# Mixture-of-experts layer: expert rows scaled by their gates and added by indirect transfers to two DRAM buffers, in place of a gather and combine stage

## The reference, cut to what matters

```python
h = tok(...)                                # (8, 256, 256), a state-space kernel
h = concatenate([h, txt], axis=1)           # (8, 768, 256)
h = h + attn(layernorm(h), Wq, Wk, Wv, Wo)
h = h + ffn(layernorm(h), Wr, br, W1, b1, W2, b2)

def ffn(x, ...):                            # 8 experts, the best 2 per token
    logits = xf @ Wr + br
    topk_w, topk_idx = top_k(logits, 2)
    topk_w = softmax(topk_w)
    gate = sum(one_hot(topk_idx, 8) * topk_w[..., None], axis=1)
    y = relu(xf @ W1[e] + b1[e]) @ W2[e] + b2[e]     # for each expert e
    return einsum('te,eth->th', gate, y)
```

## Time and profile before

| | us |
|---|---|
| median of 3 runs | 2702.7 |
| lowest and highest | 2696.3, 2704.53 |
| profiled execution, its own time | 2709.06 |
| span of that execution, first to last instruction | 2707.3 |

### The profile page before, as it was taken

How to read it: one execution, slowest core, us unless ns; L and a number is a source line. 1 busy time by engine, 2 the same in 40 slices (tenths; PEclk the granted TensorE clock), 3 DMA queues, 4 the chain that set the end, 5 groups by cost and what they waited for, 6 DMA issues and landing times. The chain is left out here.

```text
span 2707.3 us, 59046 instructions
## 1 busy us (share of the span) xinstructions
PE 2210.2 (82%) x20292; PEld 1180.7 (44%) x20293; DVE 1780.5 (66%) x2903; ACT 1052.7 (39%) x2156; POOL 808.8 (30%) x752
## 2 busy tenths in 40 slices
PE   0458998998998998998998999886996699999900
PEld 0433343343343343443343343335885466666600
DVE  8438888888888878978978988962545222222223
ACT  1025555555555645655655555531111122222200
POOL 0042523523523523433433342200344000000076
PEclk6578999999999999999999999998997799999955
DMA  2222342342342333333333324316774211111144
GB/s 43 56 78 50 96 112 68 94 106 73 95 104 72 98 90 87 98 82 94 94 82 91 89 81 98 86 49 202 238 253 146 68 62 61 62 62 62 55 133 146
DMA packets 216852, 258.20 MB, mean 95 GB/s; under 512 B 57248, under 2 KB 181664, under 8 KB 216608
## 3 DMA queue, kind: packets, MB, share of 16 engines
q1 hardware_dynamic: 186016, 209.84, 29.0%
q0 software_dynamic: 9216, 25.18, 2.8%
q10 hardware_dynamic: 21376, 19.93, 2.2%
HBM read 105.40 MB, written 61.34 MB: 62 GB/s over the span
## 5 line engine op out<-in xcount | busy, mean ns | idle before, releaser
L631 ACT ACTIVATE a_prob<-ps_s,a_nmax 128x768 f32<-128x768 f32 x768 | 692.4, 902 | 743.2 <-DVE a_nmax L749 721.3
L749 DVE TENSOR_REDUCE a_nmax<-ps_s 128x1 f32<-128x768 f32 x768 | 718.2, 935 | 238.4 <-PE ps_s L561 231.9
L561 PE MATMUL ps_s<-a_kT,a_qT 64*128 64x384 f32 x3072 | 677.5, 535 | 129.4 <-ACT a_prob L631 102.7
L755 DVE STREAM_TRANSPOSE a_probT<-a_prob 128x768 f32<-128x768 f32 x768 | 735.9, 962 | 0.0
L568 PE MATMUL ps_o<-a_probT,a_vrep 32*64 32x384 f32 x12288 | 574.3, 500 | 38.7 <-ACT a_xnext L619 15.6
L561 PEld LDWEIGHTS ps_s<-a_kT,a_qT 64*128 64x128 f32 x3072 | 241.3, 188 | 538.2 <-ACT a_prob L631 359.2
L568 PEld LDWEIGHTS ps_o<-a_probT,a_vrep 32*64 32x64 f32 x12288 | 248.1, 134 | 334.7 <-issue 138.6
L695 POOL TENSOR_TENSOR a_o<-a_o,a_invrow 128x1536 f32<-128x1536 f32 x32 | 110.1, 3442 | 811.1 <-ACT a_o L639 811.1
L444 POOL TENSOR_TENSOR a_prod<-a_raw,a_table 128x384 f32<-128x384 f32 x312 | 302.3, 1001 | 31.7 <-ACT a_raw L623 24.5
L1355 POOL DMA_INDIRECT c_yg<-ys_d,c_idx x96 | 93.2, 971 | 497.3 <-DVE c_idx L1322 468.4
L1275 DVE TENSOR_TENSOR e_h<-ps_eh,eb 128x512 f32<-128x512 f32 x104 | 71.9, 692 | 234.6 <-PE ps_eh L1205 233.5
(11 more groups left out here) (202 smaller groups left out, 1574.0 us busy)
## 6 DMA issues: line engine op xcount, KB each, us to landing
a_qT<-a_qp SPq DMA_DIRECT2D x512, 96.0 KB, 3.7
a_vrep<-a_vraw SPq DMA_DIRECT2D x512, 48.0 KB, 2.0
a_invrow<-inv_d SPq DMA_DIRECT2D x64, 384.0 KB, 4.9
oT_d<-a_o SPq DMA_DIRECT2D x32, 768.0 KB, 3.3
r_oT<-oT_d SPq DMA_DIRECT2D x192, 128.0 KB
e_x<-xs_d SPq DMA_DIRECT2D x104, 128.0 KB, 2.0
ys_d<-e_y ACTq DMA_DIRECT2D x104, 128.0 KB, 1.7
ew<-in_L_ffn_W_dram SPq DMA_DIRECT2D x16, 512.0 KB
```

Source lines behind the costliest of these rows:

```text
L561: last = pe.matmul(S[:, s % 2, r, 0:HALF], qT[rows, par, 2 * hp + c, P * t:P * t + P], kT[rows, par, :], start=True, stop=True)
L631: act.activation(prob[:, s % RING, :].rearrange("p (r k) -> p r k", r=2), S[:, s % 2, :, 0:HALF], ACT.Exp, bias=nmax[:, s % RING:s % RING ...
L749: v.tensor_reduce(nmax[:, s % RING:s % RING + 1], S[:, s % 2, :, 0:HALF], AX.XY, ALU.max, negate=True).then_inc(max_ready, 1)
L755: v.transpose(turned(par, s), prob[:, s % RING, :]).then_inc(t_ready, 1)
```

## The change

`combine`, `ys_d`, `pos`, `gate`, `move` and `renumber` go. In their place:

- A row of `xs_d` gets 8 more columns (`DX = D + 8`): the token's number, its two experts, its two gates. `place` writes them beside `xn`, and the scatter carries them along. The filler rows carry rows beyond the last token and experts that no tile has.
- `acc_d` and `acc2_d` are two new DRAM buffers of 6144 + 128 rows. ACT stores `h1` to `acc_d` at the end of each batch in `route`. GpSimd writes zeros to `acc2_d` in `vandermonde`, 8 transfers of 768 KB.
- In `experts` DVE works out each row's gate and destination (`gates`) and multiplies the row by it, in a second operation after the bias. GpSimd adds the tile with an indirect transfer with `compute_op=add`, even tiles to `acc_d`, odd ones to `acc2_d`. Each waits for the one before it on the same buffer. SP's load of a tile waits for the gates as well.
- A last block copies `acc_d` to the output by 8 DRAM to DRAM transfers on SP and adds `acc2_d` onto it by 8 more on GpSimd (`accum_op=add`), each after the copy of its batch.

```diff
@@ vandermonde, GpSimd
+                pool.memset(zero[:], 0.0).then_inc(zero_ready, 1)
+                pool.wait_ge(zero_ready, 1)
+                pool.wait_ge(loaded_c, 16 * NB)
+                for b in range(NB):
+                    pool.dma_start(acc2_d[SEQ * b:SEQ * b + SEQ, :].rearrange("(p t) d -> p (t d)", p=P), zero[:]).then_inc(zeroed, 16)
+                pool.wait_ge(zeroed, 16 * NB)
@@ route
-        xn = sb("r_xn", [P, 2, TT, D])
+        xn = sb("r_xn", [P, 2, TT, DX])
                 sp.wait_ge(zeroed, 16 * NE)
+                sp.wait_ge(h_stored, 16 * NB)
...
-                pool.memset(zeros[:], 0.0).then_inc(const, 1)
+                pool.memset(pads[:], 0.0).then_inc(const, 1)
+                pool.memset(xn[:, :, :, D + 5:DX], 0.0).then_inc(const, 1)
+                pool.iota(tok_i[:], [[SEQ, NB], [P, TT]], base=0, channel_multiplier=1).then_inc(const, 1)
+                pool.wait_ge(const, 6)
+                pool.memset(pads[:, D + 1:D + 1 + TOPK], -2.0).then_inc(const, 1)
+                pool.iota(pads[:, D:D + 1].bitcast(I32), [[0, 1]], base=TOK, channel_multiplier=1).then_inc(const, 1)
...
+                def store(b):
+                    act.wait_ge(h1_ready, b * TT + (TT + 3))
+                    act.dma_start(acc_d[bass.ds(b * SEQ, SEQ), :].rearrange("(t p) d -> p t d", p=P), h1[:, b]).then_inc(h_stored, 16)
...
                     root(b)
+                    store(b)
...
-                    v.tensor_copy(gate[:, b, 0, :], gr[:])
-                    v.tensor_tensor(gate[:, b, 1, :], ex[:], gr[:], ALU.mult)
+                    v.tensor_copy(xn[:, q, :, D].bitcast(I32), tok_i[:, b, :])
+                    v.tensor_copy(xn[:, q, :, D + 1:D + 1 + TOPK], top[:])
+                    v.tensor_copy(xn[:, q, :, D + 3], gr[:])
+                    v.tensor_tensor(xn[:, q, :, D + 4], ex[:], gr[:], ALU.mult)
...
-                    k.mark(v.tensor_copy(pos[:, b, :, :], posf[:]))
@@ tile_table
-    mark(v.tensor_scalar(move[:], cnt[:], float(P), -float(STRIDE), ALU.mult, ALU.add))
+    link(v.tensor_scalar(ind[:], j[:], last[:], None, ALU.is_gt))
+    mark(v.scalar_tensor_tensor(out=held_by[:], in0=ind[:], scalar=-2.0 * NE, in1=e[:], op0=ALU.mult, op1=ALU.add))
@@ experts
-                        sp.wait_ge(xt_done, j + 1)
+                        hold(sp, xt_done, j + 1)
+                        hold(sp, gate_ready, j + 1)
                         load(j + RING, n)
...
-                def store(j, n):
-                    act.wait_ge(y_ready, j + 1)
-                    act.dma_start(ys_d[j], y[:, n, :]).then_inc(stored[n], 16)
...
+            @block.gpsimd
+            def _(pool):
+                def tile(j, n):
+                    hold(pool, y_ready, j + 1)
+                    q = n % 2
+                    if not (isinstance(j, int) and j < 2):
+                        hold(pool, added[q], (j >> 1) * 16)
+                    pool.indirect_dma_start(out=(acc_d, acc2_d)[q], out_offset=bass.IndirectOffsetOnAxis(ap=row_i[:, n:n + 1], axis=0),
+                                            in_=y[:, n, :], in_offset=None, compute_op=ALU.add).then_inc(added[q], 16)
+
+                loop(pool, tile)
+                for q in range(2):
+                    pool.wait_ge(added[q], NT // 2 * 16)
...
-                    wait(v, stored[n], (j >> 2) * 16)
-                    v.tensor_tensor(y[:, n, :], Y[:, q, 0:D], b2[:, bass.ds(ex, 1), :].rearrange("p o f -> p (o f)"), ALU.add).then_inc(y_ready, 1)
+                    v.tensor_tensor(y[:, n, :], Y[:, q, 0:D], b2[:, bass.ds(ex, 1), :].rearrange("p o f -> p (o f)"), ALU.add).then_inc(bias_ready, 1)
+                    hold(v, bias_ready, j + 1)
+                    v.tensor_scalar(y[:, n, :], y[:, n, :], gate[:, n:n + 1], None, ALU.mult).then_inc(y_ready, 1)
+
+                def gates(j, n):
+
+                    hold(v, x_in[n], (j >> 2) * 16 + 16)
+                    if not (isinstance(j, int) and j < RING):
+                        hold(v, added[n % 2], ((j - RING) >> 1) * 16 + 16)
+                    v.tensor_copy(row_i[:, n:n + 1], x[:, n, D:D + 1].bitcast(U32))
+                    v.tensor_tensor(is_it[:, n, :], x[:, n, D + 1:D + 1 + TOPK], held_by[:, bass.ds(j, 1)].to_broadcast([P, TOPK]), ALU.is_equal).then_inc(gate_dve, 1)
+                    hold(v, gate_dve, j * 2 + 1)
+                    v.tensor_tensor(share[:, n, :], is_it[:, n, :], x[:, n, D + 3:D + 3 + TOPK], ALU.mult).then_inc(gate_dve, 1)
+                    hold(v, gate_dve, j * 2 + 2)
+                    v.tensor_tensor(gate[:, n:n + 1], share[:, n, 0:1], share[:, n, 1:2], ALU.add).then_inc(gate_ready, 1)
 
                 def tile(j, n):
                     bias_h(j, n % 2)
+                    gates(j, n)
                     if not (isinstance(j, int) and j == 0):
                         bias_y(j - 1, (n - 1) % RING)
...
-                loop(v, tile, renumber)
+                loop(v, tile)
@@ program, in place of combine
+            @block.sync
+            def _(sp):
+                for b in range(NB):
+                    sp.dma_start(place(b), rows(acc_d, b)).then_inc(copied[b], 16)
+
+            @block.gpsimd
+            def _(pool):
+                for b in range(NB):
+                    pool.wait_ge(copied[b], 16)
+                    pool.dma_start(place(b), rows(acc2_d, b), accum_op=ALU.add, max_dma_last_dim=6144).then_inc(summed, 16)
+                pool.wait_ge(summed, 16 * NB)
```

More of the change, by code:

```diff
@@ L35 @@
 NT = TOK * TOPK // P + NE
+DX = D + 8
 F32 = mybir.dt.float32
@@ L112, in vandermonde @@
         stored = sem("v_stored")
+        zero = sb("v_zero", [P, SEQ // P * D])
+        zero_ready, zeroed = sem("v_zero_ready"), sem("v_zeroed")
         id_ready, known, sq_ready = sem("v_id_ready"), sem("v_known"), sem("v_sq_ready")
@@ L788, in _, with route @@
                 loop(v, iteration, drain)
-def route(nc, sem, io, ident, img_d, oT_d, xs_d, h1, pos, gate, run, base, exp_i, src_i, tail_i, move, wo, wr, br, weights, weights_in):
+def route(nc, sem, io, ident, img_d, oT_d, xs_d, acc_d, h1, run, base, exp_i, src_i, tail_i, held_by, wo, wr, br, weights, weights_in):
     w1, w2, b1, b2 = weights
@@ L1147, in experts @@
             sem(f"e_{n}") for n in ("xt_done", "xT_ready", "h_done", "h_ready", "ht_done", "hT_ready", "y_done", "y_ready"))
-        stored = [sem(f"e_stored{q}") for q in range(RING)]
+        added = [sem(f"e_added{q}") for q in range(2)]
+        gate_dve, gate_ready, bias_ready = sem("e_gate_dve"), sem("e_gate_ready"), sem("e_bias_ready")
         def wait(eng, s, value):
@@ L1152, in wait, with loop @@
                 eng.wait_ge(s, value)
-        where, moved, past = (sb(f"e_{x}", [P, NB * TOPK * TT]) for x in ("where", "moved", "past"))
-        pos_dve = sem("e_pos_dve")
-        def loop(eng, tile, between=None):
+        def loop(eng, tile):
             for n in range(RING):
                 tile(n, n)
-            if between:
-                between()
             with eng.Fori(1, NT // RING - 1) as k:
@@ L1258, in tile @@
                     relu_h(j, q)
-                    if not (isinstance(j, int) and j < 2):
-                        store(j - 2, (n - 2) % RING)
                 copy_x(0, 0)
                 loop(act, tile)
-                for n in (2, 3):
-                    store(NT - RING + n, n)
-                for n in range(RING):
-                    act.wait_ge(stored[n], NT // RING * 16)
+            @block.gpsimd
[10 more added lines that the diff above has]
+                    pool.wait_ge(added[q], NT // 2 * 16)
             @block.vector
@@ L1405, in program, with rows, place @@
             weights = (weight("ew1", [P, NE, KC, FF]), weight("ew2", [P, NE, FC, D]), weight("eb1", [P, NE, FF]), weight("eb2", [P, NE, D]))
-            route(nc, sem, io, ident, img_d, oT_d, xs_d, h1, pos, gate, run, base, exp_i, src_i, tail_i, move, wo, wr, br, weights, sem("weights_in"))
-            experts(nc, sem, ident, xs_d, ys_d, exp_i, src_i, pos, move, weights)
-        combine(nc, sem, ys_d, h1, pos, gate, out)
+            route(nc, sem, io, ident, img_d, oT_d, xs_d, acc_d, h1, run, base, exp_i, src_i, tail_i, held_by, wo, wr, br, weights, sem("weights_in"))
+            experts(nc, sem, ident, xs_d, acc_d, acc2_d, exp_i, src_i, held_by, weights)
+        with nc.Block() as block:
+            copied = [sem(f"copied{b}") for b in range(NB)]
+            summed = sem("summed")
+            def rows(d, b):
+                return d[SEQ * b:SEQ * b + SEQ, :].rearrange("(p t) d -> p (t d)", p=P)
+            def place(b):
+                return out[b].rearrange("(p t) d -> p (t d)", p=P)
+            @block.sync
[8 more added lines that the diff above has]
+                pool.wait_ge(summed, 16 * NB)
 def rotary_tables():
```

101 lines of the change are left out of this document (19 added, 82 removed).

## The result

| | before | after |
|---|---|---|
| median of the runs on one chip, us | 2699.5 | 2635.33 |
| lowest to highest | 2695.99 to 2704.53 | 2630.0 to 2639.86 |
| profiled execution, own time; span | 2709.06; 2707.3 | 2630.0; 2628.2 |

The ratio is 0.976 with a 95% interval of 0.9733 to 0.9787: faster by 64 us. The forecast was 30 us less, with 2632 to 2710 as the range.

The account below looks back on a forecast made before the run. It took GpSimd's issue to bound the combine stage at the end, with PE nearly full in experts and route. Terms -137.1 + 106 (tail) - 5 + 6 = -30 against the median 2702.7 gave 2672 us, range 2632 to 2710.

Parts of the forecast that it names:

- Combine, removed: Combine stage at the kernel's end, 96 gathers bound by GpSimd's issue at 1.25 us each: its 137.1 us go.
- Renumbering: Expert stage after tile 3: renumbering in DVE's queue delays PE; removing it gains 5 us.
- Expert stage: Added work per tile on DVE, GpSimd and SP stays hidden under the 4.12 us tile: cost nothing.
- Route: Route stage: ACT's eight stores of h1 lengthen PE's waits for r_oT, between 0 and 20 us, taken as 6.
- Drains: GpSimd's drain exposed twice: 7.9 us before the first copy, 8.2 with its barrier at the end.
- Transfers of the tail: Last block: copies 30 and additions 52 us, together 82, plus 3 for the first and last landing.
- the two cases with a second read: Last block: copies 21 us if reading and writing overlap, 41 if not; additions 42 overlapped, 62 not.
- to the first copy: Start of the tail: scaling and waits 0.5, landing 3.8, drain 7.9 and 0.5 more, 12.7 us in all.
- B: Rival for the tail: an addition costs an engine no more than a copy, transfers 42 us, not 82: 2632; chance 0.12.
- C: Rival: engines are the bound, tail transfers 103 us, not 82, h1 stores fully exposed (+14): 2707; chance 0.11.
- D: Rival: landing of additions sets the expert stage beyond 7.8 us; at 9.2, 2745; chance 0.12.
- E: Rival in the expert stage: DVE's `hold` waits overrun their cover by 0.3 us per tile, +31: 2703; chance 0.05.

Follow-up runs that it names:

- e1: The kernel before with one gather per tile of rows instead of two (48 in place of 96): 2647.19 us, ratio 0.9809.
- second group: Four follow-up kernels run on another chip, where the kernel before took 2752.89 us and their route stage 314 to 321 us.
- e2: The kernel after without the eight additions of the last block, copies only: 2601.77 us, ratio 0.9647.
- e3: The kernel after with the eight additions of the last block made plain copies on the same queue: 2622.55 us, ratio 0.9726.
- e0: The kernel after unchanged, run again as reference for its group: 2635.34 us, ratio 0.9759.

## Why the prediction was right in its direction and wrong in its size

Forecast: -137.1 + 106 - 5 + 6 = -30. By the profile's stages, without attention and the first stage: tail -137.1 + 65.0 = -72.1, renumbering -4.9, tiles +6.0, route +3.2, together -67.8. Term by term:

- **Combine, removed (-137.1).** Right, and e1 shows the mechanism: half of the gathers away, 58.0 us less.
- **Renumbering (-5).** Right. The spacing of `bias_h` at the tiles around it was 8.12 + 5.27 us before and is 4.33 + 4.19 after, 4.9 us less.
- **Expert stage (0).** The named costs were rightly hidden: the four small operations end 0.66 us after L1302, forecast 0.8 to 1.6, and DVE still idles 0.6 us ahead of L1308. The additions land in 3.8 us, the value taken, though GpSimd takes 1.55 us for an issue and not 1.25. What was missing is a resource that I did not list: register loads of PE's sequencer, which take longer where they meet the indirect transfers' packets, 6 us.

```profile
2557.88 0.69 DVE L1302 TENSOR_TENSOR e_h<-ps_eh,eb 128x512 f32<-128x512 f32 x1 [1.03 <-PE ps_eh L1228]
...
2559.07 0.16 DVE L1322 TENSOR_TENSOR e_gate<-e_share 128x1 f32<-128x1 f32 x1
2559.84 0.42 DVE L1308 TENSOR_TENSOR e_y<-ps_ey,eb 128x256 f32<-128x256 f32 x1 [0.62 <-PE ps_ey L1242]
```

- **Route (+6).** Measured +3.2, within the scatter of this stage: outside the second group the profiles give 279.4 us for before, 282.0 for e1, 276 to 286 with the change. PE's waits for r_oT are 34.4 us in all against 27.6, but in the eight profiles with the change on these chips they range from 28.3 to 35.6, without it they are 27.6 and 28.9. So the 6 us taken are neither confirmed nor refuted. No run took the stores of h1 out alone.
- **Drains (7.9 and 8.2).** The first one was rightly found in the earlier trace rows, 6.1 us. The second was hardly there (0.9 with its barrier): I took 7.9 us for a fixed cost of a block with indirect transfers and charged it to a block that has none. Both drains of 7.9 us in the rows stand behind 96 transfers; the runs show about 0.08 us for each, so the 8 direct ones cost 0.65. 7.3 us of the error.
- **Transfers of the tail (82 + 3).** This is the step that failed, in its words "the middle of the two cases with a second read, as neither case has the nearer row". Copies were put at 30 and take about 20 (21.6 us in e2 from the first issue to the last landing), additions at 52 and take 32; with landings 52.4 for 85, 32.6 us of the error. The earlier trace rows did hold the nearer row. A store of 6.29 MB is also a read and a write of each byte, only with one end in SBUF, and its 19.7 us are near the 18.8 of the copies. Halfway between overlapped and one after the other had nothing for it. For the additions even the lower of my two cases, 42 us, was too dear: a second read costs half a copy more, or a little over, not a whole one. What in the engines makes it cheaper than the first read, no run shows.

The five terms that are off, -32.6 - 7.3 - 1.1 (to the first copy) + 6 - 2.8 (route), give -37.8, which is -67.8 less -30.

That the range held is in part luck: its lower end was B's time, and the missing part of the second drain and the 6 us of the tiles stood in no term. Of the rivals, B gave 2632 and came within 3.3 us, but not by its mechanism alone: an addition does cost more than a copy (e3 against e0, 2622.55 and 2635.34). It was right that the transfers overlap, and the missing second drain paid for what it had too little. C and D fell: the DMA share in the route rose only from 0.80 to 0.86 in the stretch shown and the stage by 3.2 us, and GpSimd never waits for a landing. E fell with DVE's idle time.

## What to carry to other kernels

Where rows collected by indirect transfers are only summed, let the transfers add, and spread them over enough buffers that none waits for another's landing; a buffer takes one addition per landing and 0.7 us, 4.65 to 4.83 here. Count the transfers that GpSimd issues in a block, since its drain at the block's end takes 0.06 to 0.08 us for each: if another engine's next step waits behind that end, the time is exposed. Price a transfer between DRAM buffers from a store's row of the same bytes, and an adding one at 1.5 to 1.6 times that; store the start value where the sum must end, since a copy of the sum is a whole pass (22.7 us here). Look for what an in-order queue does without being counted as busy, such as register loads on the path, and issue them before the instruction that hides them.

## What the runs showed of the hardware

- GpSimd's DRAIN at a block's end: 0.05 us in a last block where GpSimd issues nothing (e2), and with 8 to 104 transfers in the block about 0.08 us more for each gather, scatter, indirect write or direct transfer (0.69 for 8, 4.0 for 48, 7.9 for 96, 8.6 for 104) and 0.06 for each indirect addition (6.1 for 104).
- Indirect addition of 128 rows of 1 KB: issue 1.55 us and landing 3.7 to 3.8, in a chain on one buffer 3.9 to 4.1; indirect write of the same rows 0.96 and 2.4.
- Direct additions in DRAM run at 206 to 215 GB/s in the slices where they are alone, copies at 335 by their engine time.
- PE's register load: 0.30 us, up to 0.65 where packets of an indirect transfer begin during it.
